# A transformer block and a dynamic convolution on one core: first gate ahead of the last layer norm, whole products, pair sums and late low weights on GpSimd

## The reference

```python
xn = layernorm(x)                                 # over channels
win = windows of 8 x 8 pixels
x  = x + (softmax(q k^T * scale + bias) v) w_proj # 8 heads of depth 8
x  = x + gelu(layernorm(x) w_mlp1) w_mlp2         # hidden 256
# second layer
h = pw1(x);  gap = mean(h)
scores = sigmoid(relu(gap fc1) fc2);  mask = top 32 channels of 64
h = relu(h); offsets = tanh(mean(h) off_w)        # 3 x 2 numbers an image
sel = (h * mask)[:, :32]
for i, k in enumerate((3, 5, 7)):
    w = base_k * (1 + sigmoid(offsets[i, 0])) + tanh(offsets[i, 1])
    outs.append(depthwise_conv(sel, w, k x k))
out = x + pw(concat(outs))
```

## Time and profile before

| what | value |
|---|---|
| median of 3 runs | 327.45 us (326.59 to 329.83) |
| the profiled execution, its time | 329.67 us |
| its span, first to last instruction | 327.9 us |
| mean granted clock of PE | 0.95 |
| PE busy | 273.1 us |
| DVE busy | 243.1 us |
| ACT busy | 204.5 us |
| GpSimd busy | 125.9 us |

### The profile page before, as it was taken

One profiled execution on the slowest core, in us unless ns is written; L12 is line 12 of the kernel. 1 busy time (PEld: TensorE's weight loads), 2 busy tenths in 40 slices (PEclk: granted clock), 3 DMA queues, 4 the chain that ended last, 5 costly groups with the idle time before them and its releaser, 6 DMA issues.

```text
span 327.9 us, 6733 instructions
## 1 busy us (share of the span) xinstructions
PE 273.1 (83%) x2486; PEld 215.6 (66%) x2486; DVE 243.1 (74%) x564; ACT 204.5 (62%) x331; POOL 125.9 (38%) x174
## 2 busy tenths in 40 slices
PE   1648877689999999999987999997959299699993
PEld 1335765477767676776866564552959299699992
DVE  2777376268787878888874566899885999999932
ACT  6686734728767685967636979774250754776640
POOL 5152736537687686766634513243220000000000
PEclk9987999979999999999979999998989669999998
DMA  6961385315334343425320001901247267578741
GB/s 175 202 145 38 90 195 103 81 43 110 71 92 98 77 98 75 99 70 110 92 61 2 2 0 34 202 11 43 69 80 155 52 135 140 119 156 176 162 97 32
DMA packets 35119, 31.07 MB, mean 95 GB/s; under 512 B 20816, under 2 KB 30032, under 8 KB 35088
## 3 DMA queue, kind: packets, MB, share of 16 engines
q1 hardware_dynamic: 30608, 23.55, 30.6%
q0 software_dynamic: 3392, 6.17, 11.1%
q10 hardware_dynamic: 1088, 0.94, 1.3%
HBM read 4.54 MB, written 2.10 MB: 20 GB/s over the span
## 4 chain that ended last, share of the span: by engine, by line
DVE 28%; PE 24%; POOL 18%; issue 13%; ACT 6%; SPq 5%; DMA 4%; DVEq 0%; POOLq 0%; ACTq 0%
DVE whole_w L1606 9%; POOL parts L320 8%; POOL k_blocks L537 5%; PE psum L974 5%; POOL q_blocks L545 3%; PE psum L1222 3%; SPq L432 3%; PE psum L1127 3%; PE psum L1113 2%; PE psum L895 2%; DVE conv_w L320 2%; DVE x L1638 2%; DVE whole_w L1595 2%; PE psum L993 2%; DVE whole_w L1611 2%
## 5 line engine op out<-in xcount | busy, mean ns | idle before, releaser
L1222 PE MATMUL psum<-shifted,conv_w 128*128 128x286 f32 x528 | 77.0, 307 | 11.3 <-ACT conv_w L825 7.9
L1222 PEld LDWEIGHTS psum<-shifted,conv_w 128*128 128x128 f32 x528 | 74.4, 199 | 12.9 <-issue 7.7
L974 PE MATMUL psum<-q_heads,k_blocks 128*128 128x256 f32 x384 | 62.7, 302 | 3.9 <-ACT probs L683 2.2
L974 PEld LDWEIGHTS psum<-q_heads,k_blocks 128*128 128x128 f32 x384 | 52.0, 192 | 14.9 <-ACT probs L683 6.3
L1372 DVE TENSOR_REDUCE maxima<-psum 128x8 f32<-128x512 f32 x64 | 40.4, 680 | 10.8 <-PE psum L948 10.8
L683 ACT ACTIVATE probs<-psum 128x512 f32<-128x512 f32 x64 | 37.6, 605 | 10.8 <-PE psum L974 9.7
L537 POOL DMA_DIRECT2D k_blocks<-k_parts x56 | 32.3, 584 | 6.9 <-PE psum L974 6.9
L819 ACT CAST conv_w<-whole_w 128x1408 fp32r<-128x1408 f32 x8 | 10.9, 1368 | 37.1 <-DVE whole_w L1614 37.1
L895 PE MATMUL psum<-parts,center_average 128*128 128x512 f32 x64 | 23.9, 457 | 11.3 <-DVE parts L320 7.8
L320 POOL TENSOR_TENSOR parts<-square_logvar,parts 128x512 fp32r<-128x512 f32 x14 | 20.3, 1447 | 34.0 <-ACT square_logvar L696 22.4
L948 PE MATMUL psum<-k_heads,q_blocks 128*128 128x256 f32 x128 | 25.0, 318 | 9.8 <-DMA k_heads<-k_parts 9.4
(11 more groups left out here) (144 smaller groups left out, 469.4 us busy)
## 6 DMA issues: line engine op xcount, KB each, us to landing
shifted<-images SPq DMA_DIRECT2D x32, 243.8 KB, 4.7
q_heads<-q_parts SPq DMA_DIRECT2D x128, 32.0 KB, 2.3
k_blocks<-k_parts POOLq DMA_DIRECT2D x56, 64.0 KB, 2.6
k_heads<-k_parts SPq DMA_DIRECT2D x64, 32.0 KB, 2.4
out<-x SPq DMA_DIRECT2D x8, 256.0 KB, 3.0
q_blocks<-q_parts POOLq DMA_DIRECT2D x28, 64.0 KB, 2.5
conv_w<-conv_w SPq DMA_DIRECT2D x10, 176.0 KB, 2.9
x<-in_x SPq DMA_DIRECT2D x6, 256.0 KB, 5.0
```

The lines of the kernel that those rows point to most:

```text
L974: ins = pe.matmul(bank[:, hh * G // 2:(hh + 1) * G // 2], k_blocks[:, hh, w // (NW // 2), k_part, w % (NW // 2), :], q_heads[:, w // (NW / ...
L1222: ins = pe.matmul(psum[:, CONV[bh][g], 0:SPAN], conv_w[bh][:, w_part, h * NSLOT + slot, :], shifted[:, bh, part, stream, first:first + SPA ...
```

## The change

**PE, attention's end.** In the last step `mlp1(0, range(2))` stands ahead of the variance of group 6, whose low part of the square is taken by DVE and not by GpSimd. The last group's centred values go to bank `PV` (`norm2_bank`), so that `GATE` is free for the first two pointwise products and the first gate, and the order of MLP, pointwise and gate instructions is another: the first gate's sums come after `variance2(NG - 1)` and `mlp1(3)`.

**DVE.** The first gate's steps stand before `normalise2(NG - 1)`; `pool_image` is gone; `add_mlp(4)` stands after `gate_taps(0)` and `products(0, 0)`.

**GpSimd.** `low_image` makes the pair sums too. After the images it makes the low weights of units 4 to 7.

**Whole products.** For units 0 to 3 `products` forms the products of 5 and 3 taps in two new buffers, and `add_products` adds each with one instruction. For units 4 to 7 `whole_weights_by_banks` does so with the fusing weights copied to PSUM (`fuse_bank`) and the product of 5 taps in PSUM (`product5_banks`); the pair of middle banks of the odd units changes to 6 and 7.

**ACT.** The order follows; the gate of the last two pairs stands between the moves of the third unit.

The diff, cut to what the text speaks of:

```diff
+        fuse_bank = psum[:, MLP, 320:512].rearrange("p (m c) -> p m c", c=C)
+        product5_banks = psum[:, GATE:MLP + 1, 0:320].rearrange("p h (s c) -> p h s c", c=C)
...
             def low_image(n, b4, half):
+                odd, even = (relu_out[:, half, q * G // 2:(q + 1) * G // 2] for q in range(2))
                 pool.wait_ge(S["ac_relu"], n + 1)
+                pool.wait_ge(S["po_images"], NBORDER + n)
+                pool.tensor_tensor(pair_sums[:, half, :], odd, even, ALU.add)
+                pool.tensor_tensor(pair_columns(0, b4, half), by_rows(odd), by_rows(even), ALU.add).then_inc(S["po_pairs"], 1)
                 pool.tensor_tensor(columns(1, b4, half), by_rows(relu_out[:, half, :]), columns(0, b4, half).bitcast(F32), ALU.subtract)
...
+            for u in range(4, B):
+                bh = u % 2
+                pool.wait_ge(S["ac_high"], u + 1)
+                low_part(pool, whole_w[:, bh].rearrange("p h t c -> p (h t) c"), conv_w[bh][:, 0, :, 0:C], conv_w[bh][:, 1, :, 0:C]).then_inc(S["low_weights"], 1)
...
+                if nxt is None:
+                    mlp1(0, range(2))
                 if prev is not None:
                     variance2(prev)
...
             def products(b4, bh):
-                dve.tensor_tensor(taps_window(whole_w[:, bh], 2), *factors(b4, bh), ALU.mult).then_inc(S["dv_product"], 1)
+                dve.tensor_tensor(taps_window(whole_w[:, bh], 2), *factors(b4, bh, 2), ALU.mult)
+                dve.tensor_tensor(product5[:], *factors(b4, bh, 1), ALU.mult)
+                dve.tensor_tensor(product3[:], *factors(b4, bh, 0), ALU.mult).then_inc(S["dv_product"], 1)
             def add_products(b4, bh):
...
-                for step, m in enumerate((1, 0)):
-                    dve.wait_ge(S["dv_product"], 4 * u + 1 + step)
-                    for h in range(NKT // TAP):
-                        for slot in range(TAP - KERNELS[m], TAP):
-                            tile = w[:, h, slot, :]
-                            tap = tap_w[:, m, bass.ds(2 * b4 + bh, 1), h * TAP + slot]
-                            ins = dve.scalar_tensor_tensor(tile, fuse_w[:, m, :], tap, tile, ALU.mult, ALU.add)
-                    ins.then_inc(S["dv_product"], 1)
+                dve.wait_ge(S["dv_product"], 4 * u + 1)
+                window = taps_window(w, 1)
+                dve.tensor_tensor(window, window, product5[:], ALU.add).then_inc(S["dv_product"], 1)
+                dve.wait_ge(S["dv_product"], 4 * u + 2)
+                window = taps_window(w, 0)
+                dve.tensor_tensor(window, window, product3[:], ALU.add).then_inc(S["dv_product"], 1)
+                differences(u, bh)
...
+            def whole_weights_by_banks(b4, bh):
+                u = 2 * b4 + bh
+                if u >= 6:
+                    dve.wait_ge(S["low_weights"], u - 1)
+                dve.tensor_tensor(product5_banks, *factors(b4, bh, 1, fuse_bank), ALU.mult)
+                dve.tensor_tensor(product3[:], *factors(b4, bh, 0, fuse_bank), ALU.mult)
+                dve.tensor_tensor(taps_window(whole_w[:, bh], 2), *factors(b4, bh, 2, fuse_bank), ALU.mult).then_inc(S["dv_product"], 1)
+                dve.wait_ge(S["dv_product"], 4 * u + 1)
+                middle = product5_banks[:, :, 2:5, :]
+                dve.tensor_tensor(middle, middle, product3[:], ALU.add).then_inc(S["dv_product"], 1)
+                dve.wait_ge(S["dv_product"], 4 * u + 2)
+                window = taps_window(whole_w[:, bh], 1)
+                dve.tensor_tensor(window, window, product5_banks, ALU.add).then_inc(S["dv_product"], 1)
+                differences(u, bh)
...
-            pool_image(0, 0, 0)
+            gate_means(0)
+            gate_hidden(0)
             add_mlp(2)
-            pool_image(1, 0, 1)
+            gate_scores(0)
             normalise2(NG - 1)
-            gate_means(0)
-            add_mlp(3)
             high_of_normed2(NG - 1)
-            gate_hidden(0)
+            gate_spread(0)
             for bh in range(2):
                 low_of_normed2(NG - 1, bh)
-            gate_scores(0)
-            gate_spread(0)
-            pool_image(2, 1, 0)
+            add_mlp(3)
             gate_mask(0)
+            gate_taps(0)
+            products(0, 0)
             add_mlp(4)
-            gate_taps(0)
-            pool_image(3, 1, 1)
-            products(0, 0)
-            add_mlp(5)
             add_products(0, 0)
             gate_means(1)
-            pool_image(4, 2, 0)
-            add_mlp(6)
+            add_mlp(5)
```

More of the change, by code:

```diff
@@ L304, in pointwise_bank, with norm2_bank, means_bank @@
         def pointwise_bank(n):
-            return PW1[0] if n == 0 or n % 2 else PW1[1]
+            return GATE if n < 2 else PW1[1 - n % 2]
+        def norm2_bank(c):
+            return PV if isinstance(c, int) and c == NG - 1 else NORM
+        def means_bank(k):
+            return MLP if k == 2 else GATE
         def mlp_bank(n):
@@ L554, in step @@
                     low_of_x1(pool, prev)
[L555 removed]
+                    if nxt is not None:
+                        low_of_square2(pool, prev)
                 if nxt is not None:
@@ L819, in even_high, with odd_high @@
                 act.copy(conv_w[bh][:, 0, :, 0:C], whole_w[:, bh].rearrange("p h t c -> p (h t) c")).then_inc(S["ac_high"], 1)
-            def odd_high(u, bh, moves=range(3)):
+            def odd_high(u, bh, moves=range(3), done=True):
                 act.wait_ge(S["ac_high"], u + 1)
@@ L847, in _ @@
             act.wait_ge(S["pe_pv"], 2 * NG)
+            evacuate_projection(NG - 1)
             gelu(1, 1, range(0, 2))
-            evacuate_projection(NG - 1)
+            high_of_x1(NG - 1)
             gelu(1, 1, range(2, 4))
-            high_of_x1(NG - 1)
-            gelu(2, 0, range(0, 2))
+            relu(0, 0, 0)
             square_of_centered2(NG - 1)
-            gelu(2, 0, range(2, 4))
-            relu(0, 0, 0)
+            gelu(2, 0)
+            relu(1, 0, 1)
             gelu(3, 1)
-            relu(1, 0, 1)
             load_tables(LN_AND_EXP)
@@ L860, in _ @@
             load_tables(GELU)
+            gate(0)
             gelu(4, 0)
-            gate(0)
             relu(2, 1, 0)
@@ L877, in _ @@
             keep_shared(0, 0)
-            high_weights(2, 0)
+            even_high(2, 0)
+            odd_high(2, 0, range(1), done=False)
             gate(2)
+            odd_high(2, 0, range(1, 3))
+            odd_low(2, 0)
             keep_shared(1, 1)
@@ L1023, in variance2, with mlp1 @@
                 over_channels(bank, 1).then_inc(S["pe_var2"], 1)
+            def mlp1(n, blocks=range(4)):
+                pe.wait_ge(S["dv_normed2"], 2 * n + 2)
+                for m in blocks:
+                    bh, f = m // 2, m % 2
+                    if n > 0:
+                        pe.wait_ge(S["ac_gelu"], 4 * n + m - 3)
+                    for part in range(2):
+                        ins = pe.matmul(psum[:, HIDDEN0 + m, :], mlp1_w[:, part, f * 128:(f + 1) * 128],
+                                        normed2[:, bh, bass.ds(n * G, G)], start=part == 0, stop=part == 1)
+                    ins.then_inc(S["pe_mlp1"], 1)
             def step(g, nxt, far, prev, par):
@@ L1102, in _ @@
             step(NG - 1, None, None, NG - 2, 1)
-            def mlp1(n, blocks=range(4)):
-                pe.wait_ge(S["dv_normed2"], 2 * n + 2)
-                for m in blocks:
-                    bh, f = m // 2, m % 2
-                    if n > 0:
-                        pe.wait_ge(S["ac_gelu"], 4 * n + m - 3)
-                    for part in range(2):
-                        ins = pe.matmul(psum[:, HIDDEN0 + m, :], mlp1_w[:, part, f * 128:(f + 1) * 128],
-                                        normed2[:, bh, bass.ds(n * G, G)], start=part == 0, stop=part == 1)
-                    ins.then_inc(S["pe_mlp1"], 1)
             def mlp2(n, par):
```

149 lines of the change are left out of this document (80 added, 69 removed).

## The result

The changed kernel takes 317.96 us (median of 4 runs, 316.19 to 319.39) against 327.06 (4 runs, 326.59 to 329.83): ratio 0.970 [0.963, 0.978], so 9.1 us faster. Its profiled execution took 316.19 us, with a span of 314.3. In a second comparison it was 317.15 against 328.77, ratio 0.967 [0.960, 0.974].

What follows compares the result with a forecast made beforehand. Bound: DVE's chain before the last four units. 18.6 us off, 8.8 and 3.0 on, left 6.8; plus 0.5, less 0.8 for the clock, 6.5 gained: 321.0 us, range 313.4 to 328.0.

Steps and rivals of the forecast that it cites:

- What bounds the kernel: After attention: DVE's chain to the fifth unit's weights, 71.1 us; last four units within 0.3 us of PE's time.
- Low part of square on DVE: Ahead of the last variance: about 0.55 us won there, but nothing counted from this by itself.
- First gate ahead: First gate's sums and first steps moved before the last layer norm: DVE's chain starts 2.5 us earlier.
- Pair sums, 4.4: Six images' pair sums moved from DVE to GpSimd: 4.4 us less in DVE's chain.
- Whole products, 3.0: Two products and two additions replace sixteen small instructions: 0.6 us less a unit, five units, 3.0.
- Hole of 3.51, new waits on PE: DVE's wait for gate sums queued in PE goes, 3.5 us less; DVE's new waits on PE cost 3.
- DVE's price for GpSimd: DVE's waits in the chain for 19.2 us of GpSimd's additions: 8.8 us, by the measured share of 46%.
- strict turns: DVE and GpSimd alternate, an instruction each: 14 us of DVE waits in the chain, 324.3 us; chance 0.22.
- Clock ahead of the fifth unit: 0.8 us deducted for the chance of PE's lower clock there, between 0 and 2.8.
- Rival 3: Late fifth MLP addition idles PE 4.4 us, then lower clock: slower, 329.5 us; chance 0.16 shared with Rival 4.
- Rival 4: Last four units: PSUM products and GpSimd's low weights give nothing, PE bounds; chance 0.16 shared with Rival 3.
- Rivals 1 and 2: DVE's chain: strict turns with GpSimd, 324.3 us, chance 0.22; GpSimd's additions fall into holes, 313.4 us, chance 0.17.

Runs made afterwards that it cites:

- e1: Changed kernel with the pair sums of all eight images back on DVE: 317.67 us, ratio 0.969 to the kernel before.
- f4: Changed kernel keeping only its order: pair sums on DVE, last four units as before, sixteen small instructions in every unit: 324.07 us, ratio 0.984.
- e5: Changed kernel with GpSimd's four additions an image replaced by zero fills, leaving out pair sums and low parts: 308.10 us, ratio 0.941.
- f6: f3 plus fusing weights copied to PSUM before the third unit, where products of the third and fourth units read them: 317.43 us, ratio 0.966.
- e3: Changed kernel with sixteen small instructions instead of two products and two additions in units 0 to 3: 323.30 us, ratio 0.983.
- x1: Kernel before with whole products alone, in all eight units and all in SBUF: 323.81 us, ratio 0.990.
- f3: f5 with GpSimd's fifth image held back until the first unit's weights are whole: 318.26 us, ratio 0.969.
- e4: Changed kernel with the fifth MLP addition moved ahead of gate_taps and the first unit's products: 319.79 us, ratio 0.978.
- e2: Changed kernel with the last four units by whole products in SBUF and low weights on DVE: 317.48 us, ratio 0.966.
- e6: Changed kernel, low weights of the last four units still on GpSimd, but DVE's products from and to SBUF: 319.30 us, ratio 0.980.
- f5: Changed kernel with the fifth MLP addition between gate_taps and the first unit's products: 318.77 us, ratio 0.968.

## Why the prediction was right, step by step

Forecast 321.0 us (6.5 gained), measured 317.96 (9.1): faster, as forecast, and in the range, just under the likeliest case (318 to 323.5). The direction and what bounds the kernel were right. That the sum came within 3 us is in part luck: terms were off both ways, and the gain that I gave the pair sums stood against a price for GpSimd that held much of it already. The fifth unit's weights were done at 268.33, or 271.2 with the 2.85 us of attention; I had said 273.5.

- **What bounds the kernel**: right. The gain came from DVE's chain ahead of the loop, 9.3 of 10.75 us. Little in the loop: 1.5 instead of 0.5. The term was mis-sized: I took PE's unit as 9.0 from the earlier trace rows, and it is 8.79; the timeline's joined line of two units held short waits. Before, the last units came at DVE's pace of 9.26, and three times the difference of 0.47 is 1.4 us, the 0.56 gap among it.
- **Low part of square on DVE**: forecast 0.55. From the seventh projection's start to the matmul of that variance it is 7.66 instead of 8.28 us: 0.62. The first gate's sums stand at 194.0; with the 2.85 of attention that is 197, forecast 198.
- **First gate ahead**: 2.5 forecast. The first spread comes 5.5 us earlier, of which 3.2 are left once the low parts and the MLP addition that now follow it are done. No run has this move alone.
- **Pair sums, 4.4**: the work went, its value didn't (e1). The term and part of the price for GpSimd cancel. I had cited the Trainium skill's warning (Perfetto Trace Analysis, "Optimizing Scalar/DVE Operations"); e1's -0.5 us of chain bears it out, and I gave the move a gain that it hasn't.
- **Whole products, 3.0**: 2.85 with the pair sums on DVE, 3.9 on the kernel before, 5.1 beside GpSimd's longer list (there four units, 2.4 by my price). The elements are right; of the rest 1.3 is waits for PE, and the number of instructions that can be made to wait is argued, not shown.
- **Hole of 3.51, new waits on PE**: the hole is gone; the new waits are 0.75 + 1.79 = 2.5, forecast 3.0. f4 has this move together with the others of the order, so what it is worth by itself stays open.
- **DVE's price for GpSimd**: 8.8 forecast by the share of 46%, measured 10.8 (10.5 by e5). Nearer to the share than to the 14 of strict turns: GpSimd waits as well, as its 2.05 for 1.20 shows, and some additions fall into DVE's waits. By the Trainium skill (SBUF — State Buffer, "Who interferes with whom") a DVE instruction with two inputs in SBUF and a GpSimd one that reads SBUF hold each other off, and a DVE instruction with at most one input in SBUF, outside the two-port modes, does not contend. The trace agrees: 1.82 and 1.04 us for products of 640 and 384 elements from SBUF, 0.83 and 0.55 with an operand in PSUM.
- **What was missing**: the old chain held three waits for ACT, 0.82, 0.73 and 0.77 at 210, 231 and 240 us, 2.3 in all. They vanished. Together with 0.7 of the start and 0.5 of PE's waits, less the 2.0 that I had too little for GpSimd, that is 1.5 of the 2.5 us by which the chain gained more than I said (9.3 against 6.8); the rest I can't assign.
- **Clock ahead of the fifth unit**: 0.8 off, for nothing: 1.79 us of gap and 1.00. f6, e3 and x1 show that the fear was well placed: 1.5 us, with gaps of 2.5 to 3.1.
- **Rival 3**: its hole came, somewhat smaller (3.51 us of idle for 4.4, then a clock of 0.63, fifth pointwise product at 213.3, or 216.2 with the 2.85, and not after 217); its conclusion, a loss, didn't. f3 is without the hole and gains 0.8, and e4, where it moves on, loses 2.7. At most 0.8 us was to be had there.
- **Rival 4** is true as it stands: the second half alone does nothing (e2). Rivals 1 and 2 lie at 324.3 and 313.4; the measured price for GpSimd, 10.8, is between the 14 and the 5 that they took.

## What to carry to other kernels

Work moved from VectorE to GpSimd next to a chain on VectorE comes back as waits, unless VectorE's instructions beside it have an operand in PSUM. Here it cost VectorE about half of GpSimd's time (46% before, 55% after), so don't price it at nothing. Fewer and larger instructions were worth more beside a busy GpSimd (5.1 us for four units) than beside a less busy one (2.9 for the chain's five). And before a hole of one engine is filled, look at who starts when it ends: here moving the late addition up brought GpSimd's next image into the first unit's weights, and holding that image back won 2.8 us in the profile again.

## What the hardware showed unexpectedly

- GpSimd's subtraction of 1408 elements took 5.33 and 5.49 us in two units of e6, beside a VectorE with operands in SBUF, and 3.20 beside the same products with an operand in PSUM. The wait goes both ways.
- PE's clock behind the gap ahead of the fifth unit: 1.00 in nine profiles with gaps of 1.37 to 1.91 us; 0.61 to 0.67 in four with 2.54 to 3.22 (x1, e3, f6, f4), but 1.00 in the kernel before with 2.93. And behind the 2.03 us gap ahead of the last projection, which all twelve profiles of the new order have, it was 1.00 in ten and lower in two (0.61 in f5, 0.64 in f3), with the same instructions ahead of it; this cost 1.5 to 1.7 us. What decides between the two stays open.
